# Mixture-of-experts routing with one-hot columns laid out in pairs, and gathered tiles normalised by ScalarE

## What is computed

```python
# layer 0 (hidden width 512); layer 1 (hidden 1024) has its own norm per expert and weights that sum to 1
x = x + ffn(layernorm(x))
def ffn(x):
    logits = x @ gate_w + gate_b
    probs = softmax(logits)
    top2_vals, top2_idx = top_k(probs, 2)
    # for each expert e: out += weight[:, e] * (gelu(x @ W1[e] + b1[e]) @ W2[e] + b2[e])
```

## Time and profile before

| | us |
|---|---|
| median of 3 runs | 1807.57 |
| lowest and highest | 1806.36 and 1812.35 |
| the profiled execution | 1808.58 |
| span of its profile | 1806.8 |
| TensorE busy in the span | 1691.4 (94%) |
| DVE, ACT, GpSimd busy | 976.2, 938.2, 367.1 |

### The profile page before, as it was taken

The page is one execution under the profiler, slowest core; times in us unless marked ns, Lnnn a source line. Parts: engine busy times, 40 slices in busy tenths (PEclk is TensorE's granted clock), DMA queues, the critical chain, the costliest instruction groups (busy, mean ns, idle before and its releaser), DMA issues.

```text
span 1806.8 us, 41223 instructions
## 1 busy us (share of the span) xinstructions
PE 1691.4 (94%) x13280; PEld 1550.7 (86%) x13281; DVE 976.2 (54%) x2406; ACT 938.2 (52%) x2098; POOL 367.1 (20%) x318
## 2 busy tenths in 40 slices
PE   4799999999999999598999999999999999999998
PEld 3588888878788889477999999999988999999997
DVE  4578878686523333477878888877852111111111
ACT  1143444444233334258989999899723444344433
POOL 2110000001156666330000000000102333333332
PEclk9899999998699999799999999999968999999999
DMA  9990000114178888500000000000446666666664
GB/s 160 107 172 10 10 10 9 58 39 163 50 190 199 208 210 199 176 6 20 15 15 13 15 19 13 15 19 12 154 189 191 180 185 185 174 179 185 188 174 96
DMA packets 93536, 190.33 MB, mean 105 GB/s; under 512 B 20777, under 2 KB 67625, under 8 KB 84617
## 3 DMA queue, kind: packets, MB, share of 16 engines
q1 hardware_dynamic: 60745, 139.50, 23.7%
q0 software_dynamic: 31360, 48.69, 17.2%
q10 hardware_dynamic: 1344, 1.05, 0.2%
HBM read 189.22 MB, written 33.22 MB: 123 GB/s over the span
## 4 chain that ended last, share of the span: by engine, by line
PE 52%; DVE 3%; issue 1%; ACT 1%; SPq 1%; DMA 0%; POOL 0%; ACTq 0%; DVEq 0%; POOLq 0%
PE bank L1781 24%; PE bank L2299 12%; PE bank L2338 11%; PE bank L711 1%; PE bank L714 1%; PE bank L2306 1%; ACT arena L1483 1%; PE bank L2210 1%; PE bank L2182 1%; PE bank L2189 1%; SPq L482 1%; DVE arena L1619 0%; PE bank L701 0%; DVE arena L1617 0%; PE bank L2172 0%
## 5 line engine op out<-in xcount | busy, mean ns | idle before, releaser
L1781 PE MATMUL bank<-arena 128*128 128x195 bf16 x5408 | 467.0, 248 | 15.6 <-DVE arena L1619 10.9
L1781 PEld LDWEIGHTS bank<-arena 128*128 128x128 fp8e4 x5408 | 463.8, 97 | 18.8 <-issue 17.8
L1483 ACT ACTIVATE arena<-arena,m_row 128x512 fp8e5<-128x512 f32 (+1 forms) x672 | 401.7, 678 | 44.6 <-DVE arena L1619 31.3
L2299 PEld LDWEIGHTS bank<-X,arena 128*128 128x128 f32 x2832 | 334.9, 192 | 6.2 <-issue 0.2
L2338 PE MATMUL bank<-arena,X 128*128 x1416 | 328.8, 382 | 7.4 <-issue 3.7
L2299 PE MATMUL bank<-X,arena 128*128 128x128 f32 x2832 | 335.6, 275 | 0.0
L1323 PE MATMUL bank<-arena 128*128 (+1 forms) x1352 | 312.8, 387 | 15.1 <-DVE arena L1229 15.0
L1323 PEld LDWEIGHTS bank<-arena 128*128 128x128 f32 x1352 | 253.0, 191 | 55.9 <-issue 20.9
L2338 PEld LDWEIGHTS bank<-arena,X 128*128 128x128 f32 x1416 | 260.3, 190 | 44.1 <-issue 12.8
L2414 DVE TENSOR_TENSOR arena<-bank,X 128x256 f32<-128x256 f32 x118 | 50.1, 425 | 394.6 <-PE bank L2338 362.8
L2376 ACT ACTIVATE X<-bank,arena 128x128 f32<-128x128 f32 x708 | 195.9, 379 | 67.6 <-issue 60.5
(11 more groups left out here) (253 smaller groups left out, 1476.1 us busy)
## 6 DMA issues: line engine op xcount, KB each, us to landing
arena<-m1w SPq DMA_DIRECT2D x67, 1024.0 KB, 4.8
arena<-m0w SPq DMA_DIRECT2D x67, 512.0 KB, 4.1
arena<-qd SPq DMA_DIRECT2D x25, 256.0 KB, 3.2
arena<-adjT POOLq DMA_DIRECT2D x13, 448.0 KB, 12.9
arena<-adjT POOLq DMA_DIRECT2D x13, 384.0 KB, 10.8
xs<-X SPq DMA_DIRECT2D x14, 256.0 KB, 2.7
xe<-zeros POOLq DMA_DIRECT2D x1, 3456.0 KB, 21.7
X<-x_in SPq DMA_DIRECT2D x2, 1664.0 KB, 11.6
```

The source lines that it names most:

```text
L1483: last = a.activation(self.sign[slot].bitcast(F8W)[:, q * W:q * W + nt * P], self.row[r][:, 0:nt * P], ACT.Sigmoid, scale=STEEP, bias=self ...
L1781: last = pe.matmul(bank[rb * NT + n][:, kind * KW:(kind + 1) * KW], self.split[slot][kind].bitcast(F8)[:, q * W + n * P:q * W + (n + 1) * ...
L2299: last = pe.matmul(bank[2 * s + c // 4][:, c % 4 * P:(c % 4 + 1) * P], self.W1[s][:, k * HID + c * P:k * HID + (c + 1) * P], self.rxt[s][: ...
```

## The change

In the routing, the 52 columns are taken in chunks of 14, 14, 12 and 12 (`CHUNKS` counts groups of `GROUP` = 2 columns). In memory a chunk is now: group, then place (or tile number), then the column within the pair. The elements of one column are 2 apart, and the constants need to be repeated only twice instead of 13 times. The iotas wait for the logits of 13 tiles. The idle products after a chunk are 4 and 40 in place of 6 and 36.

In the tiles, `norm` moves from DVE to ACT, with the same two steps as activations. ACT does the norms of tiles 0 and 1 at the start, of tile 2 after it has kept 0 and 1, and then that of g+3 after `keep_x` of g+2. ACT's loop body has four tiles in place of two, DVE's two in place of four.

```diff
+GROUP = 2
+CHUNKS = ((0, 7), (7, 14), (14, 20), (20, 26))
...
-                self.tile_all = words(k, flat).bitcast(BF16)[:, 0:tiles_]
+                self.tile_all = words(k, SLOT_TILES * GROUP // 2).bitcast(BF16)
...
-                self.place_all = words(k, places).bitcast(BF16)
+                self.place_all = words(k, P * GROUP // 2).bitcast(BF16)
...
-                for c in range(4):
-                    q, b = slice(c * PAIRS, (c + 1) * PAIRS), c % 2
-
-                    def row(a, n):
-                        return a.rearrange("p (o q) -> p o q", o=1).to_broadcast([P, n, PAIRS])
-                    eq = self.equal[b].rearrange("p (g q) -> p g q", q=PAIRS)
+                for c, (first, end) in enumerate(CHUNKS):
+                    groups, b = end - first, c % 2
+
+                    def columns(a, m):
+                        a = a[:, first * GROUP:end * GROUP].rearrange("p (u o r) -> p u o r", o=1, r=GROUP)
+                        return a.to_broadcast([P, groups, m, GROUP])
+
+                    def numbers(a, m):
+                        return a.rearrange("p (o m r) -> p o m r", o=1, r=GROUP).to_broadcast([P, groups, m, GROUP])
+                    eq = self.equal[b][:, 0:groups * G * GROUP].rearrange("p (u m r) -> p u m r", u=groups, r=GROUP)
                     v.wait_ge(self.hot_used[b], c // 2 + 1)
-                    v.tensor_tensor(eq, self.tile_all.rearrange("p (g q) -> p g q", q=PAIRS),
-                                    row(self.tile_of[:, q], G), ALU.is_equal).then_inc(self.hot_equal[b], 1)
+                    v.tensor_tensor(eq, numbers(self.tile_all, G), columns(self.tile_of, G), ALU.is_equal
+                                    ).then_inc(self.hot_equal[b], 1)
...
-                    for q in range(PAIRS):
-                        last = pe.matmul(bank[5][:, 0:2 * SLOT_TILES], place[:, :, q], tile[:, :, q],
-                                         start=False, stop=False, skip_group_check=True)
-                    last.then_inc(self.hot_used[c % 2], 1)
-                    idle_products(6 if c < 3 else 36)
+                    for u in range(n):
+                        for r in range(GROUP):
+                            last = pe.matmul(bank[5][:, 0:2 * SLOT_TILES], place[:, u, :, r], tile[:, u, :, r],
+                                             start=False, stop=False, skip_group_check=True)
+                    last.then_inc(self.hot_used[b], 1)
+                    idle_products(4 if c < 3 else 40)
 
             def route_gpsimd(self, pool, rows_final):
                 pool.wait_ge(*rows_final)
-                pool.iota(self.tile_all, [[1, SLOT_TILES], [0, PAIRS]], base=0, channel_multiplier=0,
+                pool.wait_ge(self.lg_done, T // 2)
+                pool.iota(self.tile_all, [[1, SLOT_TILES], [0, GROUP]], base=0, channel_multiplier=0,
                           allow_small_or_imprecise_dtypes=True).then_inc(self.places_ready, 1)
-                pool.iota(self.place_all, [[1, P], [0, PAIRS]], base=0, channel_multiplier=0,
+                pool.iota(self.place_all, [[1, P], [0, GROUP]], base=0, channel_multiplier=0,
                           allow_small_or_imprecise_dtypes=True).then_inc(self.places_ready, 1)
...
+                def norm(g, s, nth):
+
+                    x = self.rx[s]
+                    a.wait_ge(self.rx_loaded[s], 16 * nth)
+                    a.activation(slot_w[:, at(g, 1)], slot_w[:, at(g, 1)], ACT.Identity,
+                                 scale=x[:, D + 3:D + 4], bias=x[:, D + 2:D + 3])
+                    a.activation(x[:, 0:D], x[:, 0:D], ACT.Identity,
+                                 scale=x[:, D:D + 1], bias=x[:, D + 1:D + 2]).then_inc(self.rx_ready, 1)
+
+                a.wait_ge(self.slots_ready, 1)
+                for g in range(2):
+                    norm(g, g, 1)
                 a.wait_ge(self.tiles_known, 1)
...
+                norm(2, 2, 1)
                 a.wait_ge(self.b_loaded, 32)
...
                     last.then_inc(self.ht_ready[s], 1)
-                    if more:
+                    if left >= 2:
                         a.wait_ge(self.tx_ready[s], i + 3)
-                        keep_x(2 * i + s + 2, s)
...
+                        keep_x(g + 2, s)
+                    if left >= 3:
+                        norm(g + 3, (q + 3) % 4, j + 1 + (q >= 1))
...
-                v.wait_ge(self.slots_ready, 1)
-                for g in range(4):
-                    norm(g, g, 1)
                 v.wait_ge(self.tiles_known, 1)
...
-                    if not isinstance(g, int) or g + 4 < RUN_TILES:
-                        norm(g + 4, q, j + 2)
```

More of the change, by code:

```diff
@@ L2108, in route_vector @@
                     v.wait_ge(self.hot_used[b], c // 2 + 1)
[L2109 to L2110 removed]
+                    v.tensor_tensor(eq, numbers(self.tile_all, G), columns(self.tile_of, G), ALU.is_equal
+                                    ).then_inc(self.hot_equal[b], 1)
                     if c == 1:
                         weights()
[L2113 to L2115 removed]
+                    v.tensor_tensor(self.hot_place[b][:, 0:groups * P * GROUP].rearrange("p (u m r) -> p u m r", u=groups, r=GROUP),
+                                    numbers(self.place_all, P), columns(self.place_of, P), ALU.is_equal)
@@ L2116, in route_vector @@
                     v.wait_ge(self.hot_equal[b], c // 2 + 1)
-                    v.tensor_tensor(self.hot_tile[b][:, 0:PAIRS * G].rearrange("p (g q) -> p g q", q=PAIRS), eq,
-                                    row(self.codes[:, q], G), ALU.mult).then_inc(self.hot_ids[b], 1)
+                    tile = self.hot_tile[b][:, 0:groups * 2 * G * GROUP].rearrange("p (u m r) -> p u m r", u=groups, r=GROUP)
+                    v.tensor_tensor(tile[:, :, 0:G, :], eq, columns(self.codes, G), ALU.mult
+                                    ).then_inc(self.hot_ids[b], 1)
@@ L2154, in route_scalar @@
                 G = SLOT_TILES
-                for c in range(4):
-                    b = c % 2
+                for c, (first, end) in enumerate(CHUNKS):
+                    n, b = end - first, c % 2
                     a.wait_ge(self.hot_equal[b], c // 2 + 1)
                     a.wait_ge(self.hot_used[b], c // 2 + 1)
-                    last = a.activation(self.hot_tile[b][:, PAIRS * G:2 * PAIRS * G], self.equal[b], ACT.Identity,
-                                        scale=row_id[:, 0:1])
+                    tile = self.hot_tile[b][:, 0:n * 2 * G * GROUP].rearrange("p (u m) -> p u m", u=n)
+                    last = a.activation(tile[:, :, G * GROUP:2 * G * GROUP],
+                                        self.equal[b][:, 0:n * G * GROUP].rearrange("p (u m) -> p u m", u=n),
+                                        ACT.Identity, scale=row_id[:, 0:1])
                     last.then_inc(self.hot_w[b], 1)
@@ L2368, in tiles_scalar, with tile @@
                     keep_x(s, s)
+                norm(2, 2, 1)
                 a.wait_ge(self.b_loaded, 32)
-                def tile(i, s, more):
-                    e = a.value_load(expert_of[0:1, at(2 * i + s, 1)], min_val=0, max_val=E - 1)
+                def tile(j, q):
+                    g, i, s = 4 * j + q, 2 * j + q // 2, q % 2
+                    left = 4 if not isinstance(g, int) else RUN_TILES - 1 - g
+                    e = a.value_load(expert_of[0:1, at(g, 1)], min_val=0, max_val=E - 1)
                     a.wait_ge(self.h_ready[s], i + 2)
@@ L2418, in tile @@
                                     ).then_inc(self.ry_ready[s], 1)
-                    if not isinstance(g, int) or g + 4 < RUN_TILES:
-                        norm(g + 4, q, j + 2)
-                for q in range(4):
-                    tile(0, q)
-                with v.Fori(1, RUN_TILES // 4 - 1) as j:
-                    for q in range(4):
-                        tile(j, q)
-                for g in range(RUN_TILES // 4 * 4 - 4, RUN_TILES):
-                    tile(g // 4, g % 4)
+                for s in range(2):
+                    tile(0, s)
+                with v.Fori(1, RUN_TILES // 2) as i:
+                    for s in range(2):
+                        tile(i, s)
+                tile(RUN_TILES // 2, 0)
         def all_stats(v, stat):
```

51 lines of the change are left out of this document (21 added, 30 removed).

## The result

The changed kernel takes 1780.3 us (median of 4 runs, 1777.78 to 1781.51), the kernel before beside it 1806.96 us: a ratio of 0.986 with a 95% interval of 0.981 to 0.990. The profiled execution took 1780.64 us with a span of 1778.9, against 1808.58 and 1806.8 before. The forecast was 1765 in a range of 1756 to 1790: 27.9 us of the span were gained where 42.5 were summed up.

The account below looks back on a forecast made before the run. TensorE sets the end almost everywhere, with room in both routings and layer 0's tiles. Gates 23.6 + one-hot pairs 14.4 + tiles 8 - costs 3.5 = 42.5 us; 1808.6 less that, less 1.0, gives 1765 us, range 1756 to 1790.

Parts of the forecast that it names:

- (1): Routing gates, both layers: small iotas moved amid the gates end DVE's stall; 3.2 us whatever the clock does.
- (2): Routing gates: with TensorE's stop at 0.8 to 1.0 us the clock stays high; with the iota edit 23.6 us.
- The rule of the Trainium skill: Gates: a transpose doesn't count as TensorE being busy as a product does; by it the gates' sum is 3.2 us.
- The rival of a fallen clock: Gates: the granted clock falls again; chance 0.28 for both layers (1785 us), 0.22 for one (1775 us).
- (3): Routing's one-hot products: columns in pairs let DVE read at 10.3 in place of 17.57 us; 14.4 us in both layers.
- (4): Layer 0's tiles: normalising on ACT takes a tile from 3.97 to 3.82 us; 8 us, bounds nothing to 13.
- landing 3.85: Layer 0's tiles: time from a gather's start to use of its rows, 3.85 us, put into the loop of three tiles.
- the ring of three tiles: Layer 0's new loop from down products through scatter, gather, norm and Gelu: 3.63 to 3.75 us a tile, so TensorE's 3.73 binds.
- landings get denser: Layer 0's tiles: landings differ from tile to tile and get denser, so 3.82 us a tile was taken.
- the third rival: Layer 0's tiles: ACT takes DVE's place and more, slower, once landing passes 4.0 us; 1814 us at 7; chance 0.04.
- the fixed steps: Layer 0's loop of three tiles apart from the landing: 7.2 us, leaving 4.0 us for the landing at 3.73 a tile.
- (5): Stage starts, both layers: first norms on ACT, W1 beside first gathers, clock perhaps falling after idle products; cost 3.5 us in all.

Follow-up runs that it names:

- the fourth run: The kernel before with one edit: its long iotas wait until 13 tiles' logits are done; 1785.13 us, ratio 0.9877.
- run 1: The changed kernel again, unaltered, which gave its second profile; 1781.69 us, ratio 0.9859 against the kernel before.
- run 2: The changed kernel with norm and weighting of gathered tiles back on DVE, four tiles ahead; 1776.47 us, ratio 0.9831.
- the half-load pair: The changed kernel with layer 0's W1 loads at 256 KB in place of 512: norm on ACT 1773.21 us, norm on DVE 1766.83 us.
- seventh run: The changed kernel with the table of the tiles' experts made after the first one-hot group, so W1 is asked for earlier; 1779.36 us, ratio 0.9853.
- eighth run, run 8: The changed kernel with 80 idle products in place of 40 behind the last group of products; 1779.16 us, ratio 0.9853.

## Why the prediction was right, and where it was wrong

**(1) and (2), gates.** Right, 24.9 us against 23.6; counted from the stalled operation to the second pick, 12.8 and 10.2, 23.0 in all. The stall, TensorE's stop (now 0.66 us) and the clock all went as said, in both layers, and the fourth run shows that one line of waiting gives them alone. The rule of the Trainium skill that was weighed there (TensorE: Matmul & The Clock Gate, Part 4: PE-mode transpose), by which the sum would have been 3.2, was not what decided: 12 us of gates ran at 1.00 throughout in layer 0, transposes and all. The reading of it had also left out the four thin products with the gate's columns that each gate tile has beside its two idle ones. The rival of a fallen clock is refuted for the gates. Where I judged wrongly is in what else could be the cure: I treated place and length as one edit, and either is enough.

**(3), one-hot pairs.** Right, 15.1 us against 14.4. DVE's chunks cost what was worked out. For the products I took the fp32 products' 0.112 us as the nearest row; in layer 1 14 of them take 0.94 us with their tail, under 0.07 each. That was worth little, since DVE bounds the stretch. The fourth run settles that the old layout was slow at either clock, as the prediction had read it.

**(4), the norm on ACT.** Wrong, by 12.7 us, and this is the main miss. The step that failed is "landing 3.85" in the ring of three tiles. The ring was drawn rightly: in run 1 the hidden products of one tile start at 539.84 and those of the third tile after it at 551.84, 12.0 us later. But the landing was taken from one row of another order of work and held constant, with "landings get denser" as a vague allowance. It measured 4.23 us. A second term was too small as well: the fixed steps had been added up to 7.0 to 7.4 us and come to 7.7 (11.9 less the landing, in the mean of 23 tiles), most of it between the down products' start and DVE's sum. The allowance (3.82 us a tile for 3.63 to 3.75) happened to cover that, as 7.7 + 3.85 over three tiles is 3.85; it did not cover the landing. The landing is tied to the W1 load that the end of the hidden products sets off: the sooner the gather comes behind it, the longer it takes. The runs with 256 and 64 KB show it (3.75 and 3.13 us). My own condition for the third rival, a landing of more than 4.0 us, was met, and the kernel before had the signs of it: its gathers that started within 2.2 us of the hidden products' end landed after 3.84 us in the mean, the late ones after 3.17, DVE's waits for gathers 5 to 58 ended 2.9 to 4.7 us after the gathers' starts, and from 540 to 600 us the DMA engines' share was 0.84. A part of the 12.7 is something else: the one gap of 8.6 us with a fallen clock, which repeated at 8.1 in the second profile, was 6.5 with the norm on DVE (run 2) and 5.6 to 6.1 in the runs with early iotas, an early table or more idle products. In those the stretch from the first down product to the last is 230.3 to 231.5 us, against 229.9 and 230.2 with the old routing and the norm on DVE; runs 1 and 2, which differ in the norm alone, have 233.3 and 232.3. In the profiles, ACT's norm gains nothing and costs 1 to 1.6 us. What sets the wide gap off stays open.

What stays open is why DVE's placement wins 5.2 us in the medians while its one profile shows 1.3. That ACT's norm stands ahead of the next Gelu, and so puts each landing into TensorE's path, fits the half-load pair (7 us), but no run took that order away alone.

**(5), the costs.** Right in kind and undersized: 7.3 us for 3.5. W1 beside the first gathers makes the first of them longer by 1.8 us in layer 0 and 3.3 in layer 1 (seventh run, 4.76 to 2.95 and 7.1 to 3.80), where I allowed 3 at most; nearly all of the cost lies in layer 1 (6.8 of the 7.3 us). The fallen clock costs some 3 us there (eighth run), where I allowed 0 to 2. With the old one-hot layout (fourth run) the same stretches are 14.6 and 15.6 us in place of 14.9 and 22.8: 7.5 of the 15 us that pairs gain are lost right behind them.

**Against the range.** Two errors of one sign, 12.7 and 3.8 us, less 2 us of better routing, make the 15 us between 1765 and 1780. The range held it because it had been stretched for the clock rival, which did not come: that is luck.

## What to carry to other kernels

A stall of 3 us can cost four times its length if TensorE stands behind it and its clock falls; look for one-off constants that run on GpSimd while DVE has work on the critical path, and move them or make them small. The landing time of a transfer belongs to what is queued beside it, not to the transfer: before a ring is shortened by issuing it earlier, ask which load is already ahead, and read the whole spread of landings and the DMA share, not one row. When a long wait is taken out, list what it kept apart.

## What was not expected of the hardware

- Products over operands whose elements lie 26 bytes apart take 0.21 us at 1.2 GHz and at 2.4 GHz alike; with 4 bytes between them under 0.07 us at 2.4 GHz.
- Two loads of 256 KB in place of one of 512 doubled the packets. With the norm on DVE the tiles became 0.12 us longer (188 GB/s in place of 204), with the norm on ACT 0.05 us shorter (206 in place of 201).
- An iota of 1664 elements held up a tensor_scalar on 128x26 elements until its end (3.17 us in place of 0.18), while three tensor_tensor operations on as many elements took 0.20 to 0.21 us under the same iota.
- With both falls of the clock at the tile stages' starts gone (run 8), its profile has others that run 1's hasn't, among them one in the window from 928 to 934 us. Whether the one brings the other was not tried; the gain of one stretch is not yet a gain of the kernel.
